# Gathering some tiles of a graph kernel with 128 partitions instead of 125

## The reference, cut to what matters

```python
# layer 0: x is (12500, 32), row/col the sources/destinations
messages = jnp.einsum('ek,ei,kio->eo', basis, x[row], weight)
out = jnp.zeros(...).at[col].add(messages)
out = out / jnp.maximum(degree, 1.0)[:, None] + x @ root_w.T + root_b
# layer 1: features is the normed result of layer 0
R = relu(abs_distances[:, None] @ w1 + b1) @ w2 + b2
Fj = features[src]
msg = ...            # sums of R * Y(rel_vec) * Fj over components
out = jnp.zeros(...).at[dst].add(msg)
```

## Time and profile before

| | us |
|---|---|
| median of 3 runs | 9837.15 (9836.03 to 9838.02) |
| the profiled execution's own time | 9820.02 |
| its span | 9818.2 |
| POOL busy | 7750.6 (79%) |
| PE busy | 7058.8 (72%) |
| DVE busy | 6056.4 (62%) |
| ACT busy | 2782.2 (28%) |

### The profile page before, as it was taken

How to read it: one execution, slowest core, us unless ns; L and a number is a source line. 1 busy time by engine, 2 the same in 40 slices (tenths; PEclk the granted TensorE clock), 3 DMA queues, 4 the chain that set the end, 5 groups by cost and what they waited for, 6 DMA issues and landing times. The chain is left out here.

```text
span 9818.2 us, 126393 instructions
## 1 busy us (share of the span) xinstructions
PE 7058.8 (72%) x31138; PEld 3614.5 (37%) x31138; DVE 6056.4 (62%) x15302; ACT 2782.2 (28%) x6973; POOL 7750.6 (79%) x6407
## 2 busy tenths in 40 slices
PE   6555555555555555555588888888888888888888
PEld 3222222222222222222344444444444444444444
DVE  4443434344444434444488888888888888888887
ACT  1000000000000000000144444444444444444443
POOL 7777777777777777777677777787777777777786
PEclk7777677676767677777699999999999999999999
DMA  2111111111111111111122222222222222222222
GB/s 29 14 14 14 14 14 14 14 14 14 14 14 14 14 14 14 14 14 14 31 55 55 53 54 54 54 54 54 54 54 54 52 56 53 55 52 56 52 55 49
DMA packets 738237, 338.75 MB, mean 35 GB/s; under 512 B 655759, under 2 KB 672074, under 8 KB 737964
## 3 DMA queue, kind: packets, MB, share of 16 engines
q0 software_dynamic: 307200, 212.25, 13.2%
q10 hardware_dynamic: 20480, 102.42, 4.1%
q1 hardware_dynamic: 410537, 23.86, 2.9%
HBM read 324.64 MB, written 6.40 MB: 34 GB/s over the span
## 5 line engine op out<-in xcount | busy, mean ns | idle before, releaser
L170 POOL DMA_INDIRECT rows<-table_dram,idx_a x1920 | 2324.7, 1211 | 645.0 <-issue 640.1
L170 POOL DMA_INDIRECT rows<-in_x,idx_a x1920 | 2321.6, 1209 | 587.3 <-issue 587.3
L595 PE MATMUL sums_all<-shared 125*64 125x289 f32 x6400 | 2066.6, 518 | 692.2 <-issue 691.0
L472 DVE TENSOR_TENSOR shared<-own_ps,rows 125x1440 f32<-125x1440 f32 x640 | 1059.9, 1656 | 2333.0 <-DMA rows<-in_x,idx_b 1380.1
L170 POOL DMA_INDIRECT rows<-table_dram,idx_b x1280 | 1556.0, 1216 | 390.3 <-issue 385.7
L170 POOL DMA_INDIRECT rows<-in_x,idx_b x1280 | 1547.4, 1209 | 390.3 <-issue 390.3
L904 PE MATMUL sums_ps<-prods,hot 125*64 125x272 f32 x12800 | 1652.6, 405 | 185.6 <-issue 163.1
L595 PEld LDWEIGHTS sums_all<-shared 125*64 125x64 f32 x6400 | 985.3, 174 | 1589.5 <-issue 1262.0
L682 ACT ACTIVATE flat<-sums_all 64x289 f32<-64x289 f32 x640 | 261.4, 408 | 4369.6 <-PE sums_all L595 4110.9
L894 PE MATMUL radial_x<-w2p,hidden 128*125 128x384 f32 x3840 | 1410.5, 504 | 34.4 <-ACT hidden L859 34.2
L614 PE MATMUL msg_ps<-sums,wk 96*33 96x320 f32 (+1 forms) x768 | 432.6, 734 | 1359.7 <-DVE acc L481 1359.7
(11 more groups left out here) (149 smaller groups left out, 5421.6 us busy)
## 6 DMA issues: line engine op xcount, KB each, us to landing
dist_ab<-in_edge_weight ACTq DMA_DIRECT2D x128, 468.8 KB
dist_ab<-in_edge_weight ACTq DMA_DIRECT2D x128, 312.5 KB
rows<-in_x,idx_a POOLq DMA_INDIRECT x1920
rows<-table_dram,idx_a POOLq DMA_INDIRECT x1920
rows<-in_x,idx_b POOLq DMA_INDIRECT x1280
rows<-table_dram,idx_b POOLq DMA_INDIRECT x1280
vec_s<-in_edge_attr SPq DMA_DIRECT2D x129, 36.6 KB
idx_a<-in_src SPq DMA_DIRECT2D x257, 7.3 KB
```

The source lines that it names most:

```text
L170: pool.indirect_dma_start(out=rows[u][:, j, 0:width], out_offset=None, in_=table, in_offset=bass.IndirectOffsetOnAxis(ap=idx[u // 3][:, u ...
L472: dve.tensor_tensor(spread[s][:, :, 0:K].rearrange("e t (k c) -> e t k c", c=C), basis[s].unsqueeze(3).to_broadcast([EP, G, 9, C]), rows[u ...
L595: last = pe.matmul(sums_ps[s][:, 0:K + 1], hot[s][:, j, :], spread[s][:, j, :], start=(j == 0), stop=(j == G - 1))
```

## The change

Tiles 0, 2 and 4 of each unit are gathered with 128 partitions, tiles 1 and 3 with 125 as before, in both layers (`FULL_0`, `FULL_1`). So each unit has three gathers of 128 rows and two of 125. The `idx` and `rows` buffers have 128 partitions instead of 125. Partitions 125 to 127 of `idx` stand for no edge: POOL sets both buffers to zero at the start, the loads write partitions 0 to 124 alone, and the three extra rows are row 0 of the table. Nothing reads them. SP's first index loads and POOL's first gathers wait for the two memsets. All consumers read partitions 0 to 124 by name.

```diff
+FULL_0, FULL_1 = (0, 2, 4), (0, 2, 4)
...
-            "idx": [sbuf("idx_a", [EP, 3, G], I32), sbuf("idx_b", [EP, 2, G], I32)],
+            "idx": [sbuf("idx_a", [P, 3, G], I32), sbuf("idx_b", [P, 2, G], I32)],
...
-    sp.dma_start(idx[half][:, :, :], unit_edges(src, i, u0, n)).then_inc(idx_landed[half], 16)
+    sp.dma_start(idx[half][0:EP, :, :], unit_edges(src, i, u0, n)).then_inc(idx_landed[half], 16)
...
-def gather_unit(pool, table, idx, rows, width, u, gathers_begun, rows_landed):
+def gather_unit(pool, table, idx, rows, width, u, gathers_begun, rows_landed, full):
 
     pool.sem_inc(gathers_begun, 1)
     for j in range(G):
-        pool.indirect_dma_start(out=rows[u][:, j, 0:width], out_offset=None, in_=table,
-                                in_offset=bass.IndirectOffsetOnAxis(ap=idx[u // 3][:, u % 3, j:j + 1], axis=0)
+        n = P if j in full else EP
+        pool.indirect_dma_start(out=rows[u][0:n, j, 0:width], out_offset=None, in_=table,
+                                in_offset=bass.IndirectOffsetOnAxis(ap=idx[u // 3][0:n, u % 3, j:j + 1], axis=0)
                                 ).then_inc(rows_landed[u], 16)
...
-        rows = ring("rows", [EP, G, C], n=U)
+        rows = ring("rows", [P, G, C], n=U)
...
         def _(sp):
+            sp.wait_ge(idx_cleared, 2)
             for h in range(2):
                 load_indices(sp, src, idx, idx_landed, h, 0)
...
         def _(pool):
+            for h in range(2):
+                pool.memset(idx[h][:, :, :], 0).then_inc(idx_cleared, 1)
...
                 if u in (0, 3):
+                    pool.wait_ge(idx_cleared, 2)
                     pool.wait_ge(idx_landed[u // 3], 16)
-                gather_unit(pool, x, idx, rows, C, u, gathers_begun, rows_landed)
+                gather_unit(pool, x, idx, rows, C, u, gathers_begun, rows_landed, FULL_0)
...
-        rows = [sbuf(f"rows1_{n}", [EP, G, ROW]) for n in range(U)]
+        rows = [sbuf(f"rows1_{n}", [P, G, ROW]) for n in range(U)]
```

More of the change, by code:

```diff
@@ L270, in spline_layer @@
         dst_landed, nodes_landed, rw_landed, bias_landed = sem("dst_landed"), sem("nodes_landed"), sem("rw_landed"), sem("bias_landed")
-        ident_made, zeroed, spans_ready, spans_stored = sem("ident_made"), sem("zeroed"), sem("spans_ready"), sem("spans_stored")
+        idx_cleared, ident_made, zeroed, spans_ready, spans_stored = sem("idx_cleared"), sem("ident_made"), sem("zeroed"), sem("spans_ready"), sem("spans_stored")
         base_landed, span_ready, step, prep = sem("base_landed"), sem("span_ready"), sem("l0_step"), sem("prep")
@@ L473, in build @@
                                   basis[s].unsqueeze(3).to_broadcast([EP, G, 9, C]),
-                                  rows[u][:, :, :].unsqueeze(2).to_broadcast([EP, G, 9, C]), ALU.mult).then_inc(spread_ready, 1)
+                                  rows[u][0:EP, :, :].unsqueeze(2).to_broadcast([EP, G, 9, C]), ALU.mult).then_inc(spread_ready, 1)
             def add(g, u, offset):
@@ L833, in _ @@
                             pool.wait_ge(idx_landed[u // 3], (g + 1) * 16)
-                        gather_unit(pool, table_dram, idx, rows, ROW, u, gathers_begun, rows_landed)
+                        gather_unit(pool, table_dram, idx, rows, ROW, u, gathers_begun, rows_landed, FULL_1)
         @block.scalar
@@ L977, in inputs_a @@
                 tiles = bass.ds(i * (U * G) + u * G, G)
-                comp = rows[u][:, :, :].rearrange("e t (k w) -> e t k w", w=16)
+                comp = rows[u][0:EP, :, :].rearrange("e t (k w) -> e t k w", w=16)
                 dve.wait_ge(rho_ready, done(g, u))
@@ L1003, in products @@
                 dve.wait_ge(radial_ready[h], done(g, u) + CREDIT)
-                comp = rows[u][:, j0:j0 + tiles, :].rearrange("e t (k w) -> e t k w", w=16)
+                comp = rows[u][0:EP, j0:j0 + tiles, :].rearrange("e t (k w) -> e t k w", w=16)
                 ra = radial[h][:, :, 0:RA].rearrange("e t (o i) -> e t o i", i=16)
```

## The result

The change makes the kernel slower: 10523.75 us median (10499.71 to 10546.05, 4 runs) against 9837.58 us (9836.03 to 9838.22, 4 runs). The ratio is 1.0697, with a 95% interval of 1.0668 to 1.0726. The prediction was 8550 us, with a range of 8000 to 9800.

The account below looks back on a forecast made before the run. POOL, issuing gathers without a pause, was taken to bound both layers. 9820 us less 781 (layer 0) and 504 (layer 1) gave 8535; with 17 us for the runs' median 8552, stated as 8550 us, range 8000 to 9800.

Parts of the forecast that it names:

- How gathers are split: POOL's queue: 125 rows take 25 rounds over 16 engines, only 125 of 400 places carrying rows; 128 rows take 8 rounds.
- Term 1: POOL: a 128-row gather takes 0.80 us instead of 1.21, saving 0.41 us; the 0.30 us before each gather stay.
- Rows cost: Rival on POOL: real rows cost, fillers don't, so a 128-row gather takes 0.03 us more; 9948 us, chance 10%.
- fixed: Rival on POOL: a gather's time is fixed, so nothing is saved and the time stays at 9837 us; chance 5%.
- Term 2: Layer 0: POOL stays the bound, so 1,905 gathers save 0.41 us each, 781 us in all.
- Term 3: Layer 1: PE becomes the bound at 6.80 us a unit, 4352 us instead of 4856, saving 504 us.
- term 5: Start and DMA engines: two memsets delay the first gather by 1 us at most; extra rows and 16-engine landing cost nothing.
- Term 4: Layer 1: DVE's waits for late rows, about 3 us once a batch, are covered by POOL's lead and cost nothing.
- under a tenth: Sign in layer 1: DVE's wait for rows falls under a tenth of its 605 us in 4000.
- over 95: Sign in layer 1: PE's busy share is over 95%.
- landings still stall: Rival in layer 1: 3 us once a batch stay in front of PE, 384 us more; 8936 us, chance 10%.
- the one on the other side: The slower rival: each real row costs POOL time, 0.03 us more for a 128-row gather; 9948 us, chance 10%.

## Why the prediction was wrong

- *How gathers are split*: right. POOL's queue moved 245,760 packets and 210.97 MB. Of packets that is 32 for each of 5,120 gathers and 64 for layer 1's 1,280 of 125 rows, as every 125-row gather of layer 1 had before. Of bytes, with 64 for the completions, it is 1,920 x (16,384 + 64) and 1,280 x (16,000 + 1,100 + 64) in layer 0, 1,920 x (49,152 + 64) and 1,280 x (48,000 + 1,100 + 64) in layer 1: 210.97 MB, as measured. The Trainium skill, "DMA: Bandwidth & Descriptors", section "Why a DMA increments its semaphore by 16 and not by 1", has the rule: the slowest dimension is divided by the largest number up to 16 that divides it. By that rule 128 takes 16, 125 takes 5, 126 takes 14, and the counts agree: the 126-row kernel moved 16,264 bytes a gather in layer 0, which is 126 x 128, 2 x 9 fillers of 4 bytes and the 64 for the completions.
- *Term 1, the price*: right in kind, mis-sized. Rounds cost, but less: s is 1.21 - 0.944 = 0.27 us where all gathers have 128 rows and 0.25 in the change, not 0.41; the mean is near 0.96 us, not 0.80. The rule of the Trainium skill that I weighed it against ("DMA: Bandwidth & Descriptors", section "Anatomy of one DMA — SWDGE (gpsimd) path") would give s = 0, and the runs show 0.25 to 0.27. "Rows cost" and "fixed" fell, too.
- *Term 2, layer 0*: without stalls 482 us were saved, 1,905 x 0.25 = 476 by the same formula, and POOL remained the bound. With stalls 96 us are left.
- *Term 3, layer 1*: without stalls 491 us against 504 (POOL 6.81 us a unit, PE 6.77: at s = 0.25 the two bounds meet). With stalls 755 us are lost. PE's price was good (6.77 us measured, 6.80 taken) but only where nothing stalls. **This is the step that failed.** "PE turns a unit every 6.83 and 6.74 us" was read from a trace in which PE was never disturbed by gathers, and was carried over to gathers of another form as though PE's issuing had nothing to do with POOL's transfers. So did term 5, which asked of the 16 engines only their bandwidth ("busy 15% and 25%: nothing") and the order of landing.
- *Term 4, late landings*: right in part where nothing stalls. DVE's waits for rows fell from 240.7 + 69.3 to 72.4 + 62.3 us in 6000 to 8000 us (chip 13), the longest from 4.7 to 1.7 us, but not under a tenth: with POOL at 6.81 us against PE's 6.77 there is no lead to cover them, as the term itself says of that case. PE was busy 94% of layer 1's gathers, not over 95. The rival "landings still stall" was priced at 3 us a batch; its own rows give 605.4 us in 4000, 5.7 us a batch.
- *Term 5, memsets*: right; the first gather starts at 3.75 us (3.82 before).
- *The rivals*: the one on the other side was a price on POOL. None had PE stalled by what POOL's transfers do elsewhere. Nor did I ask whether the result would belong to the chip; on chips 13 and 15 the time is 8843 and 8827 us, inside the range and 3% above the forecast, most of it term 1's. There term 1's error costs layer 0 299 us (482 saved, not 781) and layer 1 at most 13.

What stays open:
- Why the kernel stalls on chips 2, 12, 14 and that of the result and not on 5, 13, 15, when the kernel before differs by under 1% between all of them. Each numbered chip ran in one set only, and that of the result has no number, so nothing shows that a chip keeps its answer from one set to another.
- What of a 128-row or 126-row gather does it (split, beat, or row 0), and by which path it reaches PE's and SP's steps from one instruction to the next.
- Whether the recording has a part. Every run has a span and a clock of its own; none shows the time without.

## What to carry over

A partition count with a large divisor up to 16 made an indirect gather cheaper for the engine that issues it (128 and 126 rows against 125); look for it when that engine is the bound. But such gathers can come with stalls on engines that have no part in them: look for "issue" on PE, for late drains and for slow register instructions on SP before trusting PE's own pace. And run such a change on several chips with the kernel before beside it: here the same program is 10% faster or 7 to 10% slower, and the repeated runs of one set agree within 0.5%.

## What the hardware showed that I had not expected

- An indirect gather's time on POOL: 25 rounds (125 rows) 1.21 us, 9 rounds (126) 0.98 to 1.00, 8 rounds (128) 0.944 behind another of its form and 0.98 behind a 125-row one. It isn't linear: from 8 to 9 rounds adds 0.04 to 0.05 us, the 16 from 9 to 25 only some 0.22.
- On chips 2, 12, 14 and the result's, PE falls to one instruction in about 0.70 us in layer 0 (in the change's trace for stretches of up to 33 us, 1.4 ms in all), and SP's loads and register instructions take the same 0.70 us; in layer 1 DVE waits up to 6.3 us for one drain (10.2 with 126 rows). POOL's, ACT's and DVE's instructions keep their durations but for a few register instructions (POOL none, DVE 5, ACT 11 over 0.6 us).
- Gathers of 125 rows can have late drains too, but few: 4 of 1,280 in the trace of the kernel before, 2 in layer 1 with four gathers on chip 12, none on chip 13.
- A memset and a wait for it on POOL cost about 0.75 us beyond the gather's own beat (2.0 against 1.25 us), most of it in front of the next gather:

```profile
2001.61 0.13 POOL L178 MEMSET pad<- 128x16 f32 x1
2002.67 1.21 POOL L173 DMA_INDIRECT rows<-in_x,idx_a  x1 [0.94 <-POOL pad L178]
```
